# First layer of a three-layer transformer step: order of the triangle products, of V's second half and of the next layer norm

## The reference, cut to what matters

```python
q = silu(x @ Wq.T).reshape(b, n, h, hd)          # 16 heads of 32
k = silu(x @ Wk.T).reshape(b, n, h, hd)
v = (x @ Wv.T).reshape(b, n, h, hd)
beta = 2.0 * jax.nn.sigmoid(x @ Wbeta.T)
k = k * jax.lax.rsqrt(jnp.sum(k * k, axis=-1, keepdims=True) + EPS)
def step(S, inp):                                  # for every token
    qt, kt, vt, bt = inp
    pred = jnp.einsum('bhk,bhkv->bhv', kt, S)
    delta = bt[..., None] * (vt - pred)
    S = S + jnp.einsum('bhk,bhv->bhkv', kt, delta)
    return (S, jnp.einsum('bhk,bhkv->bhv', qt, S))
```

## Time and profile before

| | us |
|---|---|
| median of 3 runs (5043.69 to 5046.62) | 5043.79 |
| profiled execution, its span | 5045.7 |
| TensorE busy in it | 4586.8 |
| VectorE busy in it | 3631.5 |
| a steady step of the first layer (1044.93 to 1103.60) | 58.67 |

### The profile page before, as it was taken

One profiled execution on the slowest core, in us unless ns is written; L12 is line 12 of the kernel. 1 busy time (PEld: TensorE's weight loads), 2 busy tenths in 40 slices (PEclk: granted clock), 3 DMA queues, 4 the chain that ended last, 5 costly groups with the idle time before them and its releaser, 6 DMA issues.

```text
span 5045.7 us, 144755 instructions
## 1 busy us (share of the span) xinstructions
PE 4586.8 (91%) x63104; PEld 3211.9 (64%) x63104; DVE 3631.5 (72%) x7890; ACT 2410.3 (48%) x4592; POOL 716.4 (14%) x909
## 2 busy tenths in 40 slices
PE   5799999999999998499999999999999999999998
PEld 4677777777777776356546646655654664665564
DVE  3677666676776666287787788778778778877876
ACT  3244433333333333164564565466456457546545
POOL 0000000000000000012211211221221221122121
PEclk9899999999999998699999999999999999999999
DMA  2222222222222222100000000000000000000000
GB/s 62 49 70 69 72 62 62 62 62 62 62 69 63 62 66 62 64 1 18 2 18 18 18 2 18 18 1 18 18 2 18 18 10 10 18 18 2 18 9 10
DMA packets 352135, 171.77 MB, mean 34 GB/s; under 512 B 300016, under 2 KB 300784, under 8 KB 350736
## 3 DMA queue, kind: packets, MB, share of 16 engines
q1 hardware_dynamic: 342528, 145.20, 10.8%
q10 hardware_dynamic: 8976, 17.30, 1.2%
HBM read 93.74 MB, written 67.63 MB: 32 GB/s over the span
## 4 chain that ended last, share of the span: by engine, by line
PE 43%; DVE 11%; ACT 2%; issue 1%; DMA 1%; POOL 1%; SPq 0%; DVEq 0%; ACTq 0%; POOLq 0%
PE row_psum L1682 9%; PE row_psum L1707 9%; PE row_psum L40 5%; PE row_psum L42 5%; PE row_psum L41 5%; DVE smax L1963 5%; PE row_psum L1695 4%; PE row_psum L1755 1%; DVE xr_lo L1831 1%; PE row_psum L1735 1%; DVE probs L1943 1%; PE row_psum L1473 1%; DVE stats L1797 1%; POOL rstd L1276 1%; PE row_psum L1654 1%
## 5 line engine op out<-in xcount | busy, mean ns | idle before, releaser
L1963 DVE TENSOR_REDUCE smax<-row_psum 128x1 f32<-128x512 f32 x2048 | 1270.4, 681 | 96.9 <-PE row_psum L1682 93.3
L1405 ACT ACTIVATE probs<-row_psum 128x512 f32<-128x512 f32 x2048 | 1090.7, 603 | 349.8 <-PE row_psum L1695 329.7
L1682 PE MATMUL row_psum<-k_stack,q_stack 64*128 64x512 f32 (+1 forms) x2048 | 740.3, 440 | 50.6 <-DVE smax L1963 24.5
L1695 PE MATMUL row_psum<-q_stack,k_stack 64*128 64x512 f32 (+1 forms) x2048 | 733.1, 458 | 22.3 <-ACT probs L1405 9.1
L1682 PEld LDWEIGHTS row_psum<-k_stack,q_stack 64*128 64x128 f32 (+1 forms) x2048 | 354.3, 188 | 499.5 <-DVE smax L1963 367.7
L1707 PE MATMUL row_psum<-probs,v_aug 128*32 128x512 f32 x4096 | 538.9, 603 | 1.6 <-ACT av_sb L1421 0.4
L1695 PEld LDWEIGHTS row_psum<-q_stack,k_stack 64*128 64x128 f32 (+1 forms) x2048 | 319.3, 184 | 225.8 <-ACT probs L1405 156.0
L876 DVE TENSOR_TENSOR lane_t<-lane_t,lane_p 128x30 f32<-128x30 f32 (+14 forms) x960 | 318.3, 332 | 33.0
L40 PE MATMUL row_psum<-wf_hi,xr_hi 128*128 128x320 f32 (+1 forms) x1024 | 331.9, 324 | 3.2 <-DVE xr_lo L1831 3.2
L873 DVE TENSOR_TENSOR lane_p<-lane_t 128x30 f32<-128x30 f32 (+14 forms) x960 | 315.5, 329 | 23.5
L42 PE MATMUL row_psum<-wf_hi,xr_lo 128*128 128x320 f32 (+1 forms) x1024 | 318.9, 311 | 0.0
(11 more groups left out here) (215 smaller groups left out, 10123.8 us busy)
## 6 DMA issues: line engine op xcount, KB each, us to landing
x_sp<-in_x ACTq DMA_DIRECT2D x33, 512.0 KB, 4.0
tri_dram<-tri SPq DMA_DIRECT2D x256, 64.0 KB, 2.0
lane_t<-tri_dram SPq DMA_DIRECT2D x32, 512.0 KB, 4.6
inv_dram<-lane_t SPq DMA_DIRECT2D x32, 512.0 KB, 2.6
inv_b<-inv_dram SPq DMA_DIRECT2D x256, 64.0 KB, 2.3
x_res<-in_x SPq DMA_DIRECT2D x32, 512.0 KB, 3.8
x<-x_res SPq DMA_DIRECT2D x32, 512.0 KB, 3.7
xs<-x SPq DMA_DIRECT2D x16, 1024.0 KB, 5.6
```

The lines of the kernel that those rows point to most:

```text
L1405: act.activation(probs[:, h % PROBS, tt, :], ps[:, m % STACK_BANKS, :], ACT.Exp, scale=float(DH) ** -0.5).then_inc(exp_ready, 1)
L1682: pe.matmul(ps[:, bank, :], q_stack[rows, qt, P * st:P * st + P], k_stack[rows, kv, :], start=True, stop=True).then_inc(max_mm, 1)
L1695: pe.matmul(ps[:, m % STACK_BANKS, :], k_stack[rows, kv, P * tt:P * tt + P], q_stack[rows, qt, :], start=True, stop=True).then_inc(score_m ...
L1963: dve.tensor_reduce(smax[:, g, st:st + 1], ps[:, bank_of("max", NT * g + st), :], AX.X, ALU.max).then_inc(max_ready, 1)
```

## The change

Three orders change, all in the first layer. TensorE's triangle products take the four row groups in turn, and those of the second row tile wait once, for all four masks of the first. In `step`, V's second half comes between the products of the two row tiles. On VectorE, `triangles` does one row tile, and `normalise` of the next x stands between the two. The inversion's columns of the stage `inputs`, which stood before the first part of the chain, are gone from there, and the later stages take them: three more columns stand behind the chain.

```diff
-                for e in range(HPT):
-                    if t:
-                        pe.wait_ge(tri_ready, at(b, s, TS * HPT, e + 1))
-                    rows = slice(HD * e, HD * e + HD)
-                    for g in range(KT):
-                        for half in range(2):
-                            i0 = P * t + C * half
+                if t:
+                    pe.wait_ge(tri_ready, at(b, s, TS * HPT, HPT))
+                for g in range(KT):
+                    for half in range(2):
+                        i0 = P * t + C * half
+                        for e in range(HPT):
+                            rows = slice(HD * e, HD * e + HD)
                             last = pe.matmul(bank[4 + e][C * half:C * half + C, 2 * C * g:2 * C * g + 2 * C],
                                              kq[rows, g, 0, i0:i0 + C], kq[rows, g, 0:s + 2:s + 1, i0:i0 + C],
                                              start=True, stop=True)
-                    last.then_inc(kk_ready, 1)
+                            if g == KT - 1 and half == 1:
+                                last.then_inc(kk_ready, 1)
...
                     triangles(*further, 0)
+                    project_v(*further, 1)
                     triangles(*further, 1)
-                    project_v(*further, 1)
...
-                           inputs=range(23, 26), chain0=range(26, 27), chain1=range(27, 28), chain2=range(28, 29),
-                           values=range(29, NB - 1))
+                           chain0=range(23, 24), chain1=range(24, 25), chain2=range(25, 26), values=range(26, NB - 1))
...
-                invert_ahead("inputs")
                 advance(*now, 0)
...
                 if further:
-                    triangles(*further)
+                    triangles(*further, 0)
                     normalise(*beyond)
+                    triangles(*further, 1)
```

## The result

The changed kernel is slower. Its median is 5088.05 us (5083.7 to 5110.16, 4 runs), that of the kernel before, run beside it, 5045.2 us. The ratio is 1.0088, with an interval of 1.0064 to 1.0113. The prediction said 4999 us and at most 5034, and is wrong. The profiled execution has a span of 5081.9 us, 36.2 more than the 5045.7 of the earlier trace rows.

What follows compares the result with a forecast made beforehand. TensorE's in-order stream was taken as the bound. From the profiled 5045.7 us, -40.0 in 29 first-layer steps, -8 in the chain and +2.8 in the prologue, less 1.9 to the median, gave 4999 us; range 4958 to 5034.

Steps and rivals of the forecast that it cites:

- The products, interleaved: First-layer triangle products on TensorE: 64 records with row groups in turn take 1.2 us; the first mask starts as before.
- V between the halves, `normalise` between the masks: Steady first-layer step: transposes 3.95 us after m0 (first mask's start), `solve_first` 5.0, `project_k` 7.0; the `normalise` pair takes 0.98.
- a sign that would break the prediction: In a steady step, `solve_first` waiting for `inv_b` later than 7 us after the first mask starts.
- What is late next, the way through DRAM: Transfers before `solve_third` not moved along: it starts between 16.0 and 17.7 us after the first mask, taken 17.3; saves 40.0.
- (a): From `tri` stores to `lane_t`: stores queue behind the earlier `load_x`, the load starts at 10.5, `solve_third` at 17.2 to 17.7.
- (b): Inverse's last columns, some 1.7 us, move behind the state chain; its late loads could put `solve_third` at 16.9.
- rival 3: `load_x` holds up the stores; decides once `lane_t`'s load starts at 11.5; `solve_third` 19.7, 5076 us; chance 0.05.
- Rival 2: Waits move before `solve_third` or to late loads, the clock falls there; `solve_third` 18.3, 5031 us; chance 0.18.
- The chain: State chain: with three columns fewer ahead of the first state, TensorE's 11.2 us wait for `state` mostly goes, -8 us.
- The prologue: Before the steady steps: masks wait for whole product bursts, +1.4 us for each of two spans, +2.8 us in all.

Runs made afterwards that it cites:

- the filler: The changed kernel with half of `project_q` computed once more before `solve_third`, the copy overwritten later: ratio 1.0062, median 5062.21 us.

## Why the prediction was wrong

The sum went from -45.2 us to +36.2 us, 81.4 apart. By the steps of the prediction:

**The products, interleaved: right in size, wrong in what it means.** 64 records take 1.21 us, the 1.2 that I took from the earlier trace rows. By the estimate from the figure of the Trainium skill (TensorE: Matmul & The Clock Gate, Part 3) it would have been 1.4; the trace decides for less. I had read the 5.03 us before as waits for masks. The first 64 of those records wait for nothing and take 2.48 us (timeline of before, up to 1045.8), so the order itself was most of it:

```profile
1043.52 2.48 PE L559 MATMUL span_bank<-kq 32*64 32x128 f32 x64
```

I also wrote that the products of the second tile run until m0+3.95 and, a paragraph later, that their masks begin at 3.4. Interleaved banks are all ready at the end of the burst, so the masks start at 3.92 (the idle 0.53 of the third DVE row above) and end at 6.44, not 5.85. The number stood in my own text, and I didn't carry it on.

**V between the halves, `normalise` between the masks: right.** The transposes start at 3.90 (I said 3.95), the two `normalise` instructions take 1.00 us together. `solve_first` and `project_k` are 0.4 and 0.65 us later than I said, partly for `inv_b`: in three steps `solve_first` waits for it past m0+7, which I had named as a sign that would break the prediction. The change of array mode is seen as before: 0.34 us from the first to the second matmul of V.

**What is late next, the way through DRAM: this step failed.** The load of `lane_t` was to start at 9.3 with nothing in the way and at 10.5 with (a), the load of x ahead of the stores; it started at 11.71. With (a) and (b), the late loads `inv_b`, both undone it still starts at 10.66. So the starting point was 1.36 us too early: 0.6 are the masks, and most of the rest is the last store, which I let land in 2.0 us as in the earlier trace rows and which needs 2.52 (2.63 in the mean of the kernel before). (a) and (b) together add 1.05, and (b) does it at a place that I hadn't looked at: I had it delay `solve_first`, and it also holds the stores back in SyncE's queue (the first is issued at 3.48 instead of 2.53). The load itself took 3.7 us, less than I feared, and `lane_t` landed at 15.41, where 17.3 for `solve_third` meant 14.7. The other 0.3 us are the steps in which `inv_b` came late. `solve_third` came at 18.36, not 17.3: 29 times 1.06 is 31 us of the miss. The point that I had set for rival 3, a load that starts at 11.5, was passed, though its price was not: `solve_third` isn't later than before. With (a) and (b) undone it stands at 17.06; that 17.3 would have been near for a kernel without them is luck, since the sum held part of (a).

**The clock behind the wait: at nothing in the sum, and the largest part of the miss.** Rival 2 said that the waits move and the clock falls in the new place. I gave it 0.18, as an alternative to a late `lane_t`, and priced it at 1.5 to 1.7 us in some steps against a gain of 3 in the others. It isn't an alternative. A late `lane_t` makes TensorE idle, and the idle time is what the clock falls behind. Rival 2's own place for `solve_third`, 18.3, is nearly what was measured; what came behind it, no sum of mine held. From `solve_third` to `query_corrections` the step is 1.24 us longer, 36 us in 29 steps. The 69.7 us there at the lower level cost half of themselves, 35 us, and the filler shows the cause: 1.13 of the 1.24 us go when the wait is filled.

**The chain.** I expected 8 us back from it. TensorE's wait for `state`, 11.2 us in 15 steps, is indeed gone from the waits. But from the chain's first part to `output_sums` the step takes 11.05 us instead of 10.86; what took its place I have not traced. From `query_corrections` to the next m0 the step is 33.35 us, before 33.27. That is 10 us of the miss.

**The prologue.** +7.0 us instead of +2.8. `solve_first` of the first span comes at 154.91 instead of 151.26, because the second span's products ran at the lower clock between two waits; and behind it the clock stood at the lower level for 13.65 us instead of 6.83. That is 4 us of the miss.

31, 36, 10 and 4 make the 81.

## What to carry to other kernels

When a tuned stream is shortened at one place, look for what arrives from outside it, and price the wait twice: the idle time, and the half clock behind it. Interleaving work over several buffers, as here over four banks, makes all of them ready at the end of the burst, so a consumer that took them one by one loses its overlap. Where a late arrival can't be moved, move work that depends on nothing in front of the wait; here that turned +0.9% into -0.5%, and -1.0% with one load issued later, while the same move without the wait cost 0.5%. And take the time of a transfer from the mean of many steps and not from the one that is shown: the last store landed in 2.0 us there and in 2.6 in the mean.

## What the runs showed of the hardware

- 64 records of 32x64 products with 128 columns, over four row groups in turn, take 1.21 us in every steady step; in order of row groups the same 64, without any wait, take 2.48, and 128 of them with waits 5.03. Interleaving row groups halves the burst itself.
- A 512 KB load issued just ahead of eight stores of 64 KB on another queue lengthens their way from 2.0 to 3.3 us in the median; issued later, it leaves them at 2.1. The 512 KB load behind them takes 3.5 instead of 4.7 us when the other has landed before it starts.
- Adding 3.06 us of matmuls to every step, where TensorE waited, didn't make the kernel slower; in the profiled executions the step was 1.1 us shorter: idle time of about 3 us in front of 32-row matmuls was followed by the clock's lower level in 18 of 29 steps, and work in its place in one.
- In one step, after 4.4 us without work, the clock stood at a mean of 0.69 for the next 13.5 us of full work.
